# Moving the state-by-read-out product of every second half unit from VectorE to GpSimd in a Mamba and attention block

## What is computed

```python
def step(h, inp):
    dt_t, B_t, C_t, u_t = inp
    dA = jnp.exp(dt_t[..., None] * A)
    dBu = (dt_t * u_t)[..., None] * B_t[:, None, :]
    h = dA * h + dBu
    y = jnp.einsum('bdn,bn->bd', h, C_t)
    return (h, y)
```

## Time and profile before

| | |
|---|---|
| device time, median of 3 runs | 6137.19 us |
| lowest and highest run | 6126.9 and 6150.05 us |
| profiled execution: span | 6123.8 us |
| DVE busy | 5554.8 us, 91% of the span |
| PE busy | 5309.5 us, 87% |
| ACT busy | 3780.6 us, 62% |
| POOL busy | 0.8 us, 0% |

### The profile page before, as it was taken

How to read it: one execution, slowest core, us unless ns; L and a number is a source line. 1 busy time by engine, 2 the same in 40 slices (tenths; PEclk the granted TensorE clock), 3 DMA queues, 4 the chain that set the end, 5 groups by cost and what they waited for, 6 DMA issues and landing times.

```text
span 6123.8 us, 74116 instructions
## 1 busy us (share of the span) xinstructions
PE 5309.5 (87%) x22816; PEld 3509.9 (57%) x22816; DVE 5554.8 (91%) x6069; ACT 3780.6 (62%) x9506; POOL 0.8 (0%) x8
## 2 busy tenths in 40 slices
PE   5788888888888888888889999888998989989888
PEld 3555555555555555555556655655656556556554
DVE  6999999999999999999999999998999989999962
ACT  3566666656666556666666666666666666666643
POOL 0000000000000000000000000000000000000000
PEclk7898888888888888888989988898888888889885
DMA  3211211211211211211221111111111212112100
GB/s 101 64 45 57 64 45 53 66 51 51 64 52 46 66 58 44 65 53 44 65 65 42 60 60 38 64 58 44 64 45 54 66 37 65 50 47 65 40 23 2
DMA packets 56934, 327.85 MB, mean 54 GB/s; under 512 B 13246, under 2 KB 15742, under 8 KB 23627
## 3 DMA queue, kind: packets, MB, share of 16 engines
q1 hardware_dynamic: 56490, 322.53, 16.6%
HBM read 313.52 MB, written 8.98 MB: 53 GB/s over the span
## 4 chain that ended last, share of the span: by engine, by line
PE 40%; DVE 33%; issue 20%; ACT 6%; DVEq 1%; DMA 0%; SPq 0%; ACTq 0%
DVE hs L953 12%; PE y_ps L417 10%; PE f_ps L530 7%; DVE hs L936 4%; PE f_ps L542 4%; DVE hs L957 4%; PE f_ps L581 3%; PE f_ps L496 2%; PE a_ps L455 2%; DVE neg_max L1062 2%; DVE xc L1016 2%; PE f_ps L511 2%; PE f_ps L592 2%; PE f_ps L487 2%; PE a_ps L465 1%
## 5 line engine op out<-in xcount | busy, mean ns | idle before, releaser
L953 DVE TENSOR_TENSOR_SCAN hs<-decay,hs 128x2192 f32<-128x2192 f32 x384 | 1811.1, 4717 | 28.0 <-issue 19.7
L417 PE MATMUL y_ps<-hs,ident 128*128 128x274 f32 x5376 | 1719.8, 455 | 89.5 <-issue 31.3
L715 ACT ACTIVATE decay<-dt,inner_s 128x273 f32<-128x273 f32 x3072 | 1380.6, 513 | 75.7 <-issue 40.3
L417 PEld LDWEIGHTS y_ps<-hs,ident 128*128 128x128 f32 x5376 | 1104.1, 217 | 480.8 <-issue 187.8
L936 DVE TENSOR_TENSOR hs<-b_rows,dtu 128x2192 f32<-128x2192 f32 x384 | 935.5, 2436 | 99.2 <-PE y_ps L417 76.7
L957 DVE TENSOR_TENSOR hs<-hs,c_rows 128x2192 f32<-128x2192 f32 x384 | 934.7, 2434 | 3.4
L530 PE MATMUL f_ps<-qk 16*92 16x274 f32 x2304 | 733.5, 458 | 227.9 <-ACT hid L788 216.4
L805 ACT ACTIVATE hid<-f_ps 92x273 f32<-92x273 f32 (+1 forms) x1152 | 421.7, 393 | 556.6 <-PE f_ps L542 552.4
L788 ACT ACTIVATE hid<-f_ps,neg_max 92x274 f32<-92x274 f32 x1152 | 544.0, 480 | 301.1 <-DVE neg_max L1062 300.9
L530 PEld LDWEIGHTS f_ps<-qk 16*92 16x92 f32 x2304 | 350.7, 174 | 549.2 <-ACT hid L788 344.6
L542 PE MATMUL f_ps<-ident,hid 92*92 92x92 f32 x3456 | 514.7, 286 | 86.8 <-ACT hid L805 48.7
(11 more groups left out here) (103 smaller groups left out, 5773.8 us busy)
## 6 DMA issues: line engine op xcount, KB each, us to landing
b_rows<-bc_rows SPq DMA_DIRECT2D x128, 1096.0 KB, 5.6
c_rows<-bc_rows SPq DMA_DIRECT2D x128, 1096.0 KB, 5.6
xp<-in_patches SPq DMA_DIRECT2D x32, 588.0 KB, 7.4
out<-h SPq DMA_DIRECT2D x32, 205.5 KB, 2.2
bc_rows<-bc_s SPq DMA_DIRECT2D x64, 34.2 KB, 1.5
h<-in_txt SPq DMA_DIRECT2D x32, 57.8 KB, 2.3
w_in_s<-in_w_in SPq DMA_DIRECT2D x1, 1152.0 KB
fc_s<-in_fc SPq DMA_DIRECT2D x2, 576.0 KB
```

Of the source, the lines that this page charges most:

```text
L417: mm = pe.matmul(y_ps[:, 0:T], ident[:, :], hs[q % 2][:, n, :], start=(q % 2 == 0 and n == 0), stop=(q % 2 == 1 and n == end - 1))
L715: e = act.activation(decay[half][:, n, t], dt[d][:, u, t], ACT.Exp, scale=inner_s[:, d, u, s:s + 1])
L953: dve.tensor_tensor_scan(i, a, i, 0.0, ALU.mult, ALU.add).then_inc(scan_done, 1)
```

## The change

For odd q the product `hs1 * c_rows1` is left out of VectorE's program and written into GpSimd's, which was empty there. GpSimd waits for the scan of q and for the row tile, multiplies, and raises a semaphore of its own, `hc_pool`. TensorE waits for `hc_done` at even q and for `hc_pool` at odd q; SyncE does the same before it reloads `c_rows0` and `c_rows1`. The addition of neighbouring planes stays on VectorE, and since it can only follow a product of VectorE, the three paired half units are now (0, 4, 8) and no longer (0, 5, 11).

```diff
-        PAIRED = (0, 5, 11)
+        PAIRED = (0, 4, 8)
...
-                    wait(sp, (dbu_done, hc_done)[kind], anew(before, SCANS, last_scan + 1 + half, k + 4 + i))
+                    if kind == 0:
+                        wait(sp, dbu_done, anew(before, SCANS, last_scan + 1 + half, k + 4 + i))
+                    else:
+                        wait(sp, (hc_done, hc_pool)[half], anew(before, UNITS, last_scan // 2 + 1, k + 4 + i))
...
+            def odd_half(b, q):
+                pool.wait_ge(scan_done, at(b, SCANS, q + 1))
+                pool.wait_ge(bc_in[3], at(b, 32, 16 * (q // UNITS + 1)))
+                pool.tensor_tensor(hs[1][:, :, :], hs[1][:, :, :], reads[1][:, :, :], ALU.mult)\
+                    .then_inc(hc_pool, 1)
+
+            def step(b, f, e, a):
+                for q in range(1, SCANS, 2):
+                    odd_half(b, q)
...
-                    wait(pe, hc_done, at(b, SCANS, q + 1))
+                    wait(pe, (hc_done, hc_pool)[q % 2], at(b, UNITS, q // 2 + 1))
...
-                if phase == 2:
+                if phase == 2 and half == 0:
```

More of the change, by code:

```diff
@@ L228, in build @@
         hc_done = sem("hc_done")
+        hc_pool = sem("hc_done_by_pool")
         ysum = sem("ysum")
@@ L398, in _, with front, finish @@
             pool.memset(v_mask[0:1, 1:3], 0.0).then_inc(s_cp, 1)
+            def odd_half(b, q):
[6 more added lines that the diff above has]
+                    odd_half(b, q)
+            def front():
+                pass
+            def finish(f, e):
+                pass
+            program(step, pool.Fori, front, finish)
         @block.tensor
```

## The result

The changed kernel takes **6823.67 us** (median of 4 runs, 6818.12 to 6827.61) against 6132.05 us before (median of 4 runs): a ratio of 1.112, 95% interval 1.108 to 1.115. It is 692 us slower where +280 was forecast, above the range of 6100 to 6750. The sign held, and so did the first half of the mechanism, that GpSimd's product stops VectorE; what follows from the stops was sized far too small, by 407 us in all.

A forecast was written before the change was run, and what follows sets the result against it. VectorE (91% of the span) and TensorE (87%) were both taken as near their limit. Stops 3.5, additions 2.4 and gating wait 1.6 make +7.5 us a step, 240 us, plus 38 dispatch: 6417 us, range 6100 to 6750.

The forecast's parts named there:

- What GpSimd's product costs: Odd half units: one 2192-element product takes 4.9 us on GpSimd, bounds 2.4 to 6.6 us.
- One at a time: After odd scans: GpSimd's product and VectorE's operations with two SBUF operands exclude each other; chance 0.62.
- six places: Odd half units 1 to 11: shifts of the next phase 0, sum +3.5 us a step.
- dispatch: GpSimd's semaphore and start at each of 192 products: 0.2 us each, 38 us.
- VectorE goes on with operations that read PSUM or one operand: During GpSimd's product: VectorE stops only at its next two-operand operation, until the product is done; no separate size.
- In the middle the slack covers it: Half unit 7: product ends at 2514.5, before TensorE asks for it at 2517.2, so no wait.
- Come back there: 2 x 1.2: Additions moved from half units 5 and 11 to 4 and 8 cost VectorE +2.4 us a step there.
- The order at the border: Half unit 11: next image's phase 0 begins before GpSimd, ends at 2573.7, product at 2578.6; next scan +1.0 us.
- No difference in TensorE's time: Whole step: TensorE's matmul count stays the same, three paired half units before and after, costing nothing.
- A: Odd half units: both engines run side by side, VectorE never stopped, half of 467 us gained, 5903 us; chance 0.17.
- B: Border: GpSimd can't get in between back-to-back two-operand VectorE operations, +8.4 us a step, 6686 us; chance 0.13.
- C: Odd half units: GpSimd takes about 3.5 us or VectorE is slowed only in part, 6148 us; chance 0.08.

The follow-up runs named there:

- beside_product: Kernel before, plus a 128 x 1370 GpSimd product after each odd scan that nobody needs: 6435 us, ratio 1.048.
- paired048: Kernel before with only the additions moved, paired half units (0, 4, 8), all products on VectorE: 6263 us, ratio 1.021.
- the singles: Kernels with one product on GpSimd, against paired048: half unit 3 6485 us, 5 6359, 7 6356, 9 6350, 11 6234.
- only11: paired048 with only the product of half unit 11 on GpSimd: 6234 us, ratio 1.016 to the kernel before.
- only179: paired048 with the products of half units 1, 7 and 9 on GpSimd: 6495 us, ratio 1.057 to the kernel before.

## Why the prediction was wrong

**What GpSimd's product costs.** Right: 4.9 us from three rows of other instructions, 4.82 measured as median. The estimate from the Trainium skill (GPSIMD Engine Reference, Performance versus the Vector engine), 4.8, agrees as well.

**One at a time.** Right, and now shown by beside_product. It was chosen on an assumption; the rows behind it say little, since the one-operand operations in them have 274 elements (410 ns) and not 2192. The total stop of VectorE was right too. The forecast's six places, +3.5 us, hold the 2.6 us of two additions and the 14.6 us of six products that have left, so the stops in it are 20.7 us a step or 662 us, 700 with dispatch; measured are 689 us of longer durations over paired048.

**"VectorE goes on with operations that read PSUM or one operand."** Half wrong, and the step that failed first. `tensor_scalar` from SBUF to SBUF is held like a two-operand operation. It hardly alters how long VectorE stands, but it alters in front of what: at half unit 3 the affine and at half unit 5 the normalisation, both of which TensorE waits for (136 us instead of 16, and 227 instead of 130 in paired048).

**"In the middle the slack covers it."** Wrong, and the step that carries most of the miss. I had compared the product's end with the start of its own sums, and that held: TensorE waited for GpSimd 22 times in 192. What I did not follow is who waits for the VectorE operations behind the stop. At half unit 3 TensorE stands, works on at a lower clock, and since it takes its work in order the sums of the other half unit come late to phase 0. VectorE's additional idle time is 467 us; 127 of them paired048 has too, and 340 come with the products, where the forecast had 1.6 us a step or 51 us.

**"Come back there: 2 x 1.2."** Wrong, and the second part of the miss. The forecast moved the additions as VectorE's time and had them at -0.2 us a step together (+2.4 where they went, -2.6 where they left); measured are +4.1. The terms over the two profiled executions, 698 us where the forecast adds up to 278: stops 689 for 700, products gone -467 for -467, waits 340 for 51, additions moved 137 for -6.

In us a step, with the singles divided by 32; the forecast's shifts at 5 and 11 are without the addition that left there, since the measured ones are over paired048:

| place | forecast | measured |
|---|---|---|
| half unit 1 | +0.5 | +0.9 to +1.6 (by difference) |
| half unit 3 | +0.5 | +6.9 |
| half unit 5 (without the addition) | 0 | +3.0 |
| half unit 7 | +1.5 | +2.9 |
| half unit 9 | +1.3 | +2.7 |
| half unit 11 (without the addition) and the gating | +3.9 | -0.9 |
| additions moved | -0.2 | +4.1, of it 1.5 to 1.8 by the one of half unit 11 |

The forecast adds 38 us of dispatch to its column. It put TensorE's eight sums at the border into the gating. The border was too dear and the additions too cheap, and the two errors of 4 to 5 us a step cancel: that the whole is not further off is in part luck. The order at the border was wrong too: phase 0 was to begin before GpSimd, but in the changed kernel it waits 0.35 us for sums, GpSimd begins 0.27 us ahead of it, and phase 0 takes 6.86 us.

**"No difference in TensorE's time."** Wrong: the count is the same, but 403 us more go into it at 0.81 of the clock instead of 0.87. How much of the loss this is by itself was not separated from the waits that it comes with; in paired048 the matmuls already take 61 us more.

**The rivals.** A is out, the engines don't run side by side. B is out: in only11 GpSimd began its product 0.2 us before phase 0 and no place shows it shut out; its longest duration is 7.9 us, so its longest wait for VectorE some 3 us. C is out: the product takes 4.8 us and the holds are whole. The case that came, exclusion with TensorE waiting for what VectorE is held in, stood in no rival.

## What to carry to other kernels

An operation moved from VectorE to GpSimd can still take VectorE's time while both read SBUF, here 3.6 us a product for the 2.4 that were saved. To price it, list what VectorE has next, which of it is held, and who waits for that: a held operation for which nobody waits soon costs about the stop less the time saved (73 of the 93 us at half unit 7; less where a wait follows that swallows it, as at half unit 11), while two operations of together 0.75 us that TensorE waited for cost 194 us more over 32 steps. In a schedule in which two engines are busy for about 90% a seemingly neutral move (an addition from one half unit to the next) can cost 1 to 2% on its own; run it apart before the rest.

## What the runs showed of the hardware

- `tensor_scalar` from SBUF to SBUF in float32 takes 355 to 417 ns for 274 elements, little less than from PSUM (432), and is held while GpSimd multiplies, where its mean is 529 to 1357 ns. `reciprocal` of 3 elements, row maxima and operations with PSUM as one of two operands ran on with unchanged durations.
- The hold doesn't show as a wait. It lies in the duration of the held operation, on VectorE and on GpSimd (5.26 us where a `tensor_scalar` was running when the product began). A group whose duration was constant and now has a larger mean is the sign to look for. Half unit 7 of only179 has both:

```profile
2829.09 0.63 DVE L1099 TENSOR_SCALAR hid<-hid,row_inv 92x274 f32<-92x274 f32 x2
2829.15 5.26 POOL L412 TENSOR_TENSOR hs<-hs,c_rows 128x2192 f32<-128x2192 f32 x1 [91.31 <-DVE hs L980]
2829.64 4.93 DVE L1039 TENSOR_SCALAR xc<-xi,inner_s 128x274 f32<-128x274 f32 x1
```
- After 4.4 us without work TensorE did the same eight matmuls in 3.34 us that took 2.12 before, and there was a stretch of 29 us (2711 to 2740) at 0.50 of the clock.
